# Expert mixture on one Trainium2 core: down product in fp32 in place of three fp32r parts, routing weights turned one expert later

## The reference

```
scores = h @ gate_w                              # 8 experts
topk_scores, topk_idx = top_k(scores, 2)
topk_probs = softmax(topk_scores)
weight = sum(one_hot(topk_idx, 8) * topk_probs)  # zero but for two experts
g = silu(h @ w1[e]) * (h @ w2[e])                # per expert, 256 wide
out = sum over e of (g @ w3[e]) * weight[:, e]
```

## Time and profile before

| | |
|---|---|
| Time, median of 3 runs | 2327.81 us (2321.74 to 2329.93) |
| Profiled execution | 2317.44 us, span 2315.8 us |
| TensorE matmul busy | 1621.8 us, 70% of the span |
| VectorE busy | 1417.5 us, 61% |
| ScalarE busy | 1099.5 us, 47% |
| GpSimd busy | 358.5 us, 15% |
| Granted TensorE clock, mean | 0.822 of full |

### The profile page before, as it was taken

One profiled execution on the slowest core, in us unless ns is written; L12 is line 12 of the kernel. 1 busy time (PEld: TensorE's weight loads), 2 busy tenths in 40 slices (PEclk: granted clock), 3 DMA queues, 4 the chain that ended last, 5 costly groups with the idle time before them and its releaser, 6 DMA issues. The chain is left out here.

```text
span 2315.8 us, 56802 instructions
## 1 busy us (share of the span) xinstructions
PE 1621.8 (70%) x20395; PEld 1101.1 (48%) x20583; DVE 1417.5 (61%) x3148; ACT 1099.5 (47%) x2028; POOL 358.5 (15%) x346
## 2 busy tenths in 40 slices
PE   5434278888724887888553688878787888878537
PEld 2212146666523666666322365555555555555423
DVE  4763376666366877777431376666666666666646
ACT  3332235656602443344242476666666666666303
POOL 1322200000043444444321000000000000000013
PEclk8766668999956998888875699989898889899859
DMA  1115522222155121111188999989999989999441
GB/s 37 41 41 182 181 62 60 51 60 58 31 163 172 46 87 51 60 50 50 52 263 223 318 358 360 344 316 352 318 367 315 368 305 362 320 362 343 157 148 55
DMA packets 220945, 433.41 MB, mean 187 GB/s; under 512 B 54736, under 2 KB 116080, under 8 KB 211280
## 3 DMA queue, kind: packets, MB, share of 16 engines
q1 hardware_dynamic: 202928, 263.61, 37.4%
q10 hardware_dynamic: 12672, 152.05, 15.9%
q0 software_dynamic: 5088, 14.16, 2.1%
HBM read 225.93 MB, written 203.55 MB: 185 GB/s over the span
## 5 line engine op out<-in xcount | busy, mean ns | idle before, releaser
L2043 DVE CUSTOM_DVE_ANT_0 r_shifted<-r_ps_ac,r_shifted 128x512 f32<-128x512 f32 x512 | 352.2, 688 | 324.0 <-PE r_ps_ac L1920 168.1
L2009 ACT ACTIVATE r_probs<-r_ps_keys 128x512 f32<-128x512 f32 x512 | 309.1, 604 | 275.9 <-PE r_ps_keys L1927 228.1
L1927 PE MATMUL r_ps_keys<-r_ident,r_shifted 128*128 128x128 f32 x2048 | 337.5, 290 | 63.0 <-issue 18.7
L1988 ACT ACTIVATE r_wide<-r_ps_wide 128x512 f32<-128x512 f32 (+1 forms) x576 | 328.8, 590 | 77.6 <-PE r_ps_wide L1911 76.7
L1927 PEld LDWEIGHTS r_ps_keys<-r_ident,r_shifted 128*128 128x128 f32 x2048 | 275.1, 150 | 64.9 <-issue 16.5
L1911 PE MATMUL r_ps_wide<-r_r,r_qv 48*32 48x96 bf16 (+12 forms) x6144 | 238.5, 258 | 58.8 <-issue 44.5
L2051 DVE TENSOR_SCALAR r_shifted<-r_shifted,r_mx 128x512 f32<-128x512 f32 x512 | 249.2, 487 | 18.3
L873 DVE TENSOR_REDUCE c_mx<-c_ps_rows 128x2 f32<-128x256 f32 (+3 forms) x256 | 198.0, 817 | 101.7 <-PE c_ps_rows L744 101.0
L846 ACT ACTIVATE c_probs<-c_ps_keys 128x512 f32<-128x512 f32 (+1 forms) x384 | 180.5, 530 | 141.8 <-PE c_ps_keys L744 138.4
L1248 POOL TENSOR_TENSOR e_gu_half<-e_weighed,e_gu_half 128x1024 fp32r<-128x1024 f32 x64 | 155.6, 2433 | 198.6 <-ACT e_gu_half L1383 198.0
L1911 PEld LDWEIGHTS r_ps_wide<-r_r,r_qv 48*32 48x32 bf16 x6144 | 103.4, 95 | 165.3 <-issue 164.1
(11 more groups left out here) (200 smaller groups left out, 2452.9 us busy)
## 6 DMA issues: line engine op xcount, KB each, us to landing
skew<-r_wide ACTq DMA_DIRECT2D x64, 2224.0 KB, 11.8
r_shifted<-skew SPq DMA_DIRECT2D x64, 2048.0 KB, 17.2
e_weight_all<-weights SPq DMA_DIRECT2D x8, 2048.0 KB, 7.1
stack<-d_part SPq DMA_DIRECT2D x96, 128.0 KB, 2.7
stack<-b_part SPq DMA_DIRECT2D x48, 128.0 KB, 3.5
stack<-b_part POOLq DMA_DIRECT2D x48, 128.0 KB, 3.6
c_q<-stack SPq DMA_DIRECT2D x64, 96.0 KB, 2.2
c_k<-stack SPq DMA_DIRECT2D x64, 96.0 KB, 2.2
```

Source lines behind the costliest of these rows:

```text
L1927: last = pe.transpose(ps_keys[u % 2][:, j * P:(j + 1) * P], shifted[:, s, u, j * P:(j + 1) * P], ident[:, :])
L1988: act.activation(wide[:, s, c, lo:hi], ps_wide[bk % BANKS][:, 0:hi - lo], ACT.Copy).then_inc(wide_sb, 1)
L2009: act.activation(probs[:, h % 2, :, b * P:(b + 1) * P], ps_keys[u % 2][:, :].rearrange("p (j i) -> p j i", j=NT), ACT.Exp, scale=SCALE).th ...
L2043: dve.tensor_tensor_reduce(out=shifted[:, s, u, :], in0=ps_ac[u % 2][:, :], in1=shifted[:, s, u, :], scale=1.0, scalar=LOWEST, op0=ALU.add ...
```

## The change

The down product takes `weighed` and `w3` as fp32 tiles: two products an expert, one for each half, and no parts. So the tiles w3_halves and gu_halves, ScalarE's `high_product`, GpSimd's `low_product` and the split of the third weight are gone. `weighed` has four buffers in place of two, and VectorE waits, before it writes one, for the down product four experts back. TensorE waits for `weighed` itself. `turn_weights` on TensorE and `take_rows` on VectorE move from step e = 2 to e = 3; on TensorE it stands behind `turn_sums`, on VectorE ahead of `add_base`. The cut diff:

```diff
-        w3_halves = [sb(f"w3_half{i}", [P, NE, HID], F32R) for i in range(2)]
-        gu_halves = [sb(f"gu_half{i}", [P, 4, KH, L], F32R) for i in range(2)]
-        weighed = sb("weighed", [P, 2, KH, L])
+        weighed = sb("weighed", [P, 4, KH, L])
...
         @block.gpsimd
-            def low_product(m, e):
-
-                pool.wait_ge(gu_high, m + 1)
-                pool.tensor_tensor(gu_halves[1][:, e % 4, :, :], weighed[:, e % 2, :, :],
-                                   gu_halves[0][:, e % 4, :, :], ALU.subtract).then_inc(gu_low, 1)
...
                 for e in range(NE):
-                    if e + 2 < NE or ahead:
-                        low_product(NE * n + e + 2, (e + 2) % NE)
...
-            pool.wait_ge(w_high, 3)
-            pool.tensor_tensor(w3_halves[1][:, :, :], w3[:, :, :], w3_halves[0][:, :, :],
-                               ALU.subtract).then_inc(w3_low, 1)
-            low_product(0, 0)
-            low_product(1, 1)
...
         @block.tensor
             def down(m, s, e):
 
-                pe.wait_ge(gu_low, m + 1)
+                pe.wait_ge(weighed_sb, m + 1)
                 for k in range(KH):
-                    for i, (a, b) in enumerate(HALVES):
-                        last = pe.matmul(ps_o[s][:, :], w3_halves[a][:, e, k * P:(k + 1) * P],
-                                         gu_halves[b][:, e % 4, k, :], start=(e == 0 and k == 0 and i == 0),
-                                         stop=(e == NE - 1 and k == KH - 1 and i == 2))
+                    last = pe.matmul(ps_o[s][:, :], w3[:, e, k * P:(k + 1) * P], weighed[:, e % 4, k, :],
+                                     start=(e == 0 and k == 0), stop=(e == NE - 1 and k == KH - 1))
                 last.then_inc(o_ps, 1)
...
-                    if e == 2 and ahead:
+                    if e == 3 and ahead:
                         turn_weights(n + 1)
...
-            pe.wait_ge(w3_low, 1)
+            pe.wait_ge(w_loaded[2], 16)
...
         @block.scalar
-            def high_product(m, e):
-                if not isinstance(m, int) or m >= 4:
-                    act.wait_ge(o_ps, m - 3)
-                act.wait_ge(weighed_sb, m + 1)
-                act.activation(gu_halves[0][:, e % 4, :, :], weighed[:, e % 2, :, :], ACT.Copy).then_inc(gu_high, 1)
...
-                    if e + 1 < NE or ahead:
-                        high_product(NE * n + e + 1, (e + 1) % NE)
...
         @block.vector
-                if not isinstance(m, int) or m >= 2:
-                    dve.wait_ge(gu_low, m - 1)
+                if not isinstance(m, int) or m >= 4:
+                    dve.wait_ge(o_ps, m - 3)
                 dve.wait_ge(gu_sb, m + 2)
-                dve.tensor_tensor(weighed[:, e % 2, :, :], gu[:, e % 2, :, :],
+                dve.tensor_tensor(weighed[:, e % 4, :, :], gu[:, e % 2, :, :],
                                   weight_all[:, s, e, :].unsqueeze(1).broadcast_to([P, KH, L]), ALU.mult)\
                     .then_inc(weighed_sb, 1)
...
-                    if e == 2 and ahead:
+                    if e == 3 and ahead:
                         take_rows(n + 1)
...
-            for i, (w, halves) in enumerate(((w1, w1_halves), (w2, w2_halves), (w3, w3_halves))):
+            for i, (w, halves) in enumerate(((w1, w1_halves), (w2, w2_halves))):
                 dve.wait_ge(w_loaded[i], 16)
                 high(halves[0][:, :, :], w[:, :, :], w_high)
...
```

More of the change, by code:

```diff
@@ L1160, in phase_experts @@
         gu_sb = sem("gu_sb")
-        gu_high = sem("gu_high")
-        gu_low = sem("gu_low")
         hT_high = sem("hT_high")
@@ L1166, in phase_experts @@
         w_low = sem("w_low")
-        w3_low = sem("w3_low")
         w_loaded = [sem(f"w{i}_loaded") for i in (1, 2, 3)]
@@ L1408, in _ @@
             activate(1)
-            high_product(0, 0)
             steps(step, act)
@@ L1509, in _ @@
             take_rows(0)
-            for i, (w, halves) in enumerate(((w1, w1_halves), (w2, w2_halves), (w3, w3_halves))):
+            for i, (w, halves) in enumerate(((w1, w1_halves), (w2, w2_halves))):
                 dve.wait_ge(w_loaded[i], 16)
                 high(halves[0][:, :, :], w[:, :, :], w_high)
[L1513 to L1516, removed]
+                dve.wait_ge(w_high, i + 1)
+                dve.tensor_tensor(halves[1][:, :, :], w[:, :, :], halves[0][:, :, :],
+                                  ALU.subtract).then_inc(w_low, 1)
             for e in range(2):
```

## The result

The changed kernel takes 2227.14 us (median of 4 runs, 2220.66 to 2241.51) against 2328.87 of the kernel before beside it: ratio 0.9573 [0.9518, 0.9628], 102 us less where 69 were forecast. Its profiled execution took 2224.83 us; against the 2317.44 of before that is 92.6 less. I divide it at the experts phase (first up product's start to last down product's last start): it fell from 396.7 to 315.2 us, **81.5**, and everything outside it from 1919.1 to 1908.0, **11.1**. Nothing outside was edited.

The account below looks back on a forecast made before the run. TensorE was taken as nearest its bound. Six batch periods falling from 49.5 to 41.0 us give -51.3, the stretch to the last down product -17.4, sum -69: 2327.8 becomes 2259 us, range 2246 to 2280.

Parts of the forecast that it names:

- The change lies in the experts phase alone: Whole kernel: only the experts phase was read and priced, for the full -69 us; no term for other phases.
- One cooled group in every second batch, 0.7 us each batch.: TensorE, experts phase: of three half-clock stretches a batch, one remains in every second batch, adding 0.7 us to 40.3.
- Rival (a): TensorE clock keeps falling around routing: two or three groups cooled in each batch, period 43 us, 2275 us; chance 0.13.
- fp32 down product 1.77 us: TensorE, each expert: four fp32 instructions of 0.443 us replace six fp32r products of 1.40 us, +0.37 us an expert.
- Routing and turnings 3.7 us a batch: TensorE, each batch: turnings 1.1 us and routing 2.6 us, the latter down from 3.05 without ScalarE's copy ahead.
- Third weight, nothing, at best 1 us: Third weight's high and low parts go; TensorE waited 0.3 us once for the low part; nothing counted, at best 1 us.
- GpSimd slows VectorE: VectorE, experts phase: without GpSimd's low products, weighing falls 2.22 to 1.23 us, one-hot rows 3.68 to 1.65, norm's end 3.22 to 1.12.
- The wait for the turned weights goes whatever they cost: TensorE, each batch: turning one expert later removes the 5.22 us wait for routing weights, whatever VectorE's weights cost.
- (b): VectorE becomes the bound, slow for reasons other than GpSimd: period 46.0 us, 40 of 69 us lost, 2299 us; chance 0.05.
- (c): Routing weights land late by DMA, over 14 us rather than 7.1; 2 us beyond gives 2273 us; chance 0.02.
- (d): Slower: fp32 down products at half clock, 0.89 us an instruction, 2372 us; decision point 0.71 an instruction; chance 0.03.
- (e): No effect, if TensorE's time in the experts phase were not on the path; chance 0.03.

Follow-up runs that it names:

- Experiments 8 to 11: Unused TensorE increments added: changed kernel, four behind each down product, 2250.39 us; kernel before, 64 ahead of relative loop, 2312.78; changed kernel, 192 ahead, 2264.73; 192 behind, 2254.25.
- experiments 3 and 4: Changed kernel with the old parts computed again but unused, 2292.6 us; changed kernel with a spare GpSimd subtraction behind each weighing, 2227.72 us.
- experiment 3: Changed kernel with ScalarE's high copies, GpSimd's low products and the third weight's parts computed again, read by no TensorE product: 2292.6 us, ratio 0.9857.
- experiment 2: Changed kernel with the turning of the weights and the copy of their rows back at step 2: 2237.11 us, ratio 0.9608.
- experiment 6: Changed kernel with the second half of each down product left out: 2184.2 us, ratio 0.9369.

## Why the prediction was wrong

Inside the experts phase the mechanism was right and the sizes were somewhat small; outside it the prediction had nothing. By its steps:

- *"The change lies in the experts phase alone"*, and so the sum had no term for any other. **This step failed.** The relative phase is 7 to 23 us shorter (885.8 and 896.1 before; 878.7 and 873.1 after), because the changed kernel's shorter list on TensorE puts the same loop elsewhere among the blocks of 16384 bytes. Over all kernels this is worth some 20 us (the table's last column), and that is what the medians leave outside the experts phase. Experiments 8 to 11 show that the place of the loop in TensorE's list decides, not the work and not the list's length. Five or six fetches more in the phase (117 against 112 or 111) go with it in every kernel; how they cost some 4 us each stays open.
- *One cooled group in every second batch, 0.7 us each batch.* None is cooled: the clock is 1.00 from 737 to 1032 us. The routing is still a stretch with a wait of 0.87 in it, seven times, and the clock held through each. Rival (a) did not happen for the same reason.
- *fp32 down product 1.77 us.* It is 1.72 alone, and 4.51 an expert where 4.57 was forecast. The row of the later phase was the right one to take; the correction to its eight instructions was too small. By the four passes that the Trainium skill (FP8 and Floating Point Precision, TensorE Precision Notes) states, it would have been 1.87, an estimate with 0.233 us a pass. The trace lies 0.15 below; if there are four passes, one costs 0.215 us here.
- *Routing and turnings 3.7 us a batch.* They are 39.39 - 8 x 4.51 = 3.3.
- These three explain the batch: 0.70 + 0.48 + 0.4 is 1.6 below the forecast 41.0, and 39.39 was measured. Six periods gained 61.0 instead of 51.3; the tail (974.56 to 1040.88, 66.3 us) gained 19.4 instead of 17.4, for one more batch of the same and eight down products.
- *Third weight, nothing, at best 1 us.* The first up product to the first gate product is 1.25 us shorter. 69 + 9.7 + 2.0 + 1.25 gives the 81.5 but for 0.5 of rounding.
- *GpSimd slows VectorE.* Right, for the weighing (1.225), the one-hot rows (1.65) and the norm's end (1.11), and experiments 3 and 4 show it by overlap. The prediction had read the form of it from one row, 1.65 us until GpSimd ends and then 1.08; experiment 3 shows it 48 times.
- *The wait for the turned weights goes whatever they cost.* Right; without the move it would be 1 us seven times (experiment 2), not 5.
- *Rivals.* (b) did not happen: TensorE waits for no gated product. (c) did not: the weights land 7.7 us after their issue (median, kernel after),

```profile
e_weight_all<-weights SPq DMA_DIRECT2D x8, 2048.0 KB, 7.7
```

and VectorE never waits for them. (d): 0.429 us an instruction is far from 0.71. (e): experiment 6 shows TensorE's time on the path.

The range reached 13 us below the forecast, for sizes inside the phase, and took nothing for the rest of the program. The 12.9 us of missed sizes alone would have given 2246, its low end. The 19 us from there to the measured 2227 lie outside the experts phase, where the prediction had no term.

## What to carry to other kernels

A GpSimd operation that nobody waits for is not free when it runs beside VectorE: read the same VectorE instruction's duration with and without GpSimd beside it, and price the removal by that. Here the price of one meeting is what is left of the GpSimd operation when VectorE's begins, however small VectorE's own work is. TensorE taking a slower form (1.72 for 1.40 us) pays where it removes such an overlap. When a kernel's list of instructions changes in length, compare the fetch count and the lengths of phases that were not edited before crediting the edit with the whole difference. The median of the runs less the edited phase tells this better than one profiled execution.

## What the runs showed of the hardware that I had not expected

- A phase with a loop of 6 iterations runs about 20 us longer, of some 880, in kernels with five or six more fetches of 16384 bytes in it, and 64 idle instructions ahead of it are enough to change that.
- Semaphore increments on TensorE are free behind down products of a bound TensorE (phase 315.3 with 256 of them) and cost 0.13 us each where nothing hides them (25.0 us for 192).
- The rows of a mixed fp32 and fp32r sequence must be read together. The first up product behind an fp32 down product shows 1.96 us for its six instructions instead of 1.56, and starts 1.31 us after the down product, whose four instructions alone take 1.72. As the ends are modelled, only the sum of 4.51 means something.
- Several VectorE operations that begin beside a GpSimd operation end only after it: a weighing 1.09 us after it, a cast of 128x32 0.03 after it (1.42 us against 0.18). Gated products that read PSUM and the MAX8 and index searches are not held.
